# A two-layer network on groups of four row tiles: 512 rows stream in layer 1, layer 2's quantised weights stay in DRAM and come in half-column passes

## The chip, the cores and the metric

The kernel runs on one core of a Trainium2 chip. TensorE (PE in the profile) multiplies matrices, with PEld its weight loads; VectorE (DVE), ScalarE (ACT) and GpSimd (POOL) do the element-wise work, and SyncE's queue (SP) issues the DMAs. The metric is the device time in microseconds from the first to the last instruction, median of three runs.

## The reference, cut to what matters

```python
def mx_quant(x):                      # blocks of 32 along the last axis share one exponent
    amax = max(abs(block)); scale = exp2(floor(log2(amax)) - 6)
    return clip(round(x / scale), -128, 127) * scale
def mx_linear(x, W, b): return bf16(mx_quant(x) @ mx_quant(W).T + b)
def ffn(inputs):                      # rows of 1024, hidden 4096
    x = bf16(inputs)
    h = layernorm(x) * ln_w + ln_b    # rounded to bf16
    h = mx_linear(h, W1, b1)          # layer 1: 1024 -> 4096
    h = gelu(h)                       # tanh form, rounded to bf16
    h = mx_linear(h, W2, b2)          # layer 2: 4096 -> 1024
    return bf16(x + h)
x = x + tanh(g_xattn) * mixer(ctx, layernorm(x))      # 4096 rows, long convolution per head
x = x + tanh(g_ffn) * ffn(layernorm(x))
```

The hidden row has to be complete before it can be quantised, because the blocks of layer 2's contraction run over all of the 4096 hidden values as they are laid out here (32 chunks of 128 partitions, one hidden value of each chunk in a block). So a group's layer 2 can start only when its last hidden chunk has been through gelu, the maxima and the quantising.

## The kernel before

There are 32 tiles of 128 rows. `mixer_block` computes the convolution part, writes the 32 tiles of x1 to DRAM, quantises layer 2's weights (W2) and stores them in DRAM (`store_w2`, L228), and prepares the input of the first four tiles (`EARLY`) for layer 1. It ends near 1029 us. `ffn_block` then runs the network on groups of `GROUP` = 2 tiles, 16 groups of 256 rows. Everything is written out by hand: each engine has its own list of instructions in a fixed order, and semaphores join the lists. No scheduler moves anything.

- **TensorE**: `layer1(g, b)` (L961) computes two of 32 hidden chunks, each with 8 matmuls of 256 streamed columns, into one of four PSUM buffers (`L1_BANKS`). `layer2(t, part)` (L976) takes the quantised hidden tile as stationary operand and streams 512 columns of the resident W2; 64 matmuls a tile, 128 a group. The first two groups' layer 1 is interleaved with a lag of 11 buffers (`LAG`), then comes layer 2 of group 0, layer 1 of group 2, layer 2 of group 1, and so on: a group's layer 1 stands one group ahead of layer 2.
- **ScalarE**: `add_bias` (L1022) empties PSUM, `gelu` (L1029) works on quarters of the hidden tile (128 x 2048 elements), `first_norm` (L1001) normalises the input of a later tile, `norm_again` (L1009) the residual.
- **VectorE**: W1's 16 weight tiles are quantised while the first layer 1 runs (`weight_ints` L1199, `weight_scales` L1203, `weight_clip` L1208, `weight_quant` L1213); tile j releases hidden chunks 2j and 2j+1. `peak` (L1134 to L1146) takes the maxima of a quarter, `hidden_scales` and three instructions (L1162, L1167, L1172) quantise a group, `first_statistics` (L1065 to L1078), `second_statistics`, `weigh_input` and `quantise_input` (L1094 to L1124) make a later tile's input, `second_bias` and `gated_sum` (L1180, L1183, L1189) finish a tile of output.
- **GpSimd**: one or two tiny powers and products per tile (L1268, L1270), between `first_statistics` and `first_norm`.
- **SP queue**: W1's raw tiles through six places, W2 once into `w2_T` (8 MB, resident), x1 tiles, the transposing DMAs of the inputs (`turn_input`), output stores.

At the head of each list stands what the next group needs. Two places of the lists matter below. In VectorE's weight loop the maxima wait for gelu:

```python
                if j in (7, 11):
                    peak(0, j // 4 - 1)
```

and on ScalarE each group's list ends with the norms of the tiles two groups on, ahead of the next group's `add_bias`:

```python
                for s in range(GROUP):
                    if g + 2 < groups:
                        first_norm(GROUP * (g + 2) + s)
```

## Time and profile before

| | us |
|---|---|
| median of three runs | 1991.64 (1991.03 to 1994.72) |
| the profiled execution | 1993.12 |
| its span in the trace | 1991.2 |
| first layer 1 matmul starts | 1031.5 |
| last layer 2 matmul ends | 1984.9 |
| PE busy, DVE busy, ACT busy | 1900.2 (95%), 1695.3 (85%), 755.8 (38%) |

A row of the page's groups names line, engine and operation, output and inputs, count, busy time and mean duration. In the trace's timeline each row has start, duration and, in brackets, how long the engine sat idle and who released it. The chain that ended last lists start and length of each link. PEclk is the granted TensorE clock, 1.00 is 2.4 GHz and 0.50 is 1.2 GHz; a value in between is a mean over the stretch.

### The profile page before, as it was taken

To read this page: it belongs to the slowest core of one execution; us is meant where nothing else is said; L and a number is where in the kernel's file an instruction comes from. 1 tells how busy PE (TensorE), PEld (TensorE's weight loads), DVE (VectorE), ACT (ScalarE), POOL (GpSimd) and SP (SyncE) were. 2 spreads that over 40 slices of the span, in tenths; PEclk is the share of its full clock that TensorE was granted. 3 is DMA by queue.
4 is the path that set the end of the run, shared out by engine and by line. 5 is a ranking of instruction groups with operands and counts; after the bars stand their busy time and mean duration, and the time that the engine had idled before them with its cause. 6 is when DMAs were issued, how large, how long until landed. Compare 5 with 4: busy or idle time off the path is not lost. (4 is left out here: it accounts for less than half of the span.)

```text
span 1991.2 us, 29456 instructions
## 1 busy us (share of the span) xinstructions
PE 1900.2 (95%) x11632; PEld 1499.2 (75%) x11680; DVE 1695.3 (85%) x2082; ACT 755.8 (38%) x1036; POOL 955.9 (48%) x1028
## 2 busy tenths in 40 slices
PE   6999999999999999999966959999999999999998
PEld 5988888888898988899854736667777666666773
DVE  6899999998898888988889798988888888898843
ACT  4333333333334333333303524444554444445440
POOL 3888899888899999999940000000000000000000
PEclk9999999999999999999978979999999999999999
DMA  6554445665645554655448312212221212211112
GB/s 247 186 179 157 156 155 202 210 224 217 220 173 168 183 195 153 217 175 193 144 174 321 129 43 75 75 49 69 75 75 69 70 53 64 75 61 57 54 43 74
DMA packets 99274, 271.75 MB, mean 136 GB/s; under 512 B 41472, under 2 KB 41472, under 8 KB 90944
## 3 DMA queue, kind: packets, MB, share of 16 engines
q1 hardware_dynamic: 99136, 269.86, 39.4%
q8 instruction: 92, 1.51, 0.3%
q14 instruction: 46, 0.38, 0.1%
HBM read 218.91 MB, written 42.53 MB: 131 GB/s over the span
## 5 line engine op out<-in xcount | busy, mean ns | idle before, releaser
L318 PE MATMUL y_ps<-kk_hi,slab 128*128 128x352 f32 (+6 forms) x3328 | 895.4, 351 | 21.7 <-DMA slab<-taps_scratch 18.4
L318 PEld LDWEIGHTS y_ps<-kk_hi,slab 128*128 128x128 f32 x3328 | 595.2, 189 | 90.4 <-issue 22.4
L318 PE MATMUL y_ps<-kk_lo,slab 128*128 128x512 f32 (+6 forms) x1664 | 580.9, 349 | 0.0
L976 PE MATMUL acc_ps<-w_T,arena 128*128 128x512 bf16 x2000 | 439.5, 379 | 2.5
L961 PE MATMUL l_ps<-f_xq_T,w_T 128*128 128x256 bf16 x3584 | 399.1, 275 | 21.4 <-ACT arena L1022 16.7
L961 PEld LDWEIGHTS l_ps<-f_xq_T,w_T 128*128 128x128 bf16 x3584 | 353.1, 99 | 68.3 <-ACT arena L1022 17.0
L976 PEld LDWEIGHTS acc_ps<-w_T,arena 128*128 128x128 bf16 x2048 | 200.3, 98 | 238.6
L1268 POOL TENSOR_TENSOR f_rstd<-f_var_eps,f_neg_half 128x1 f32<-128x1 f32 x28 | 15.3, 548 | 706.6 <-DVE f_var_eps L1078 706.6
L318 PEld LDWEIGHTS y_ps<-kk_lo,slab 128*128 128x128 f32 x1664 | 314.2, 189 | 34.2
L1022 ACT ACTIVATE arena<-l_ps,f_b 128x256 bf16<-128x256 f32 x512 | 213.8, 472 | 246.6 <-PE l_ps L961 241.2
L509 DVE TENSOR_TENSOR upper<-y_ps,q_ext 128x768 f32<-128x768 f32 (+1 forms) x128 | 156.0, 1218 | 96.5 <-PE y_ps L318 90.8
L748 POOL TENSOR_TENSOR lsum<-lower 128x240 f32<-128x240 f32 x127 | 169.1, 1332 | 65.8 <-DVE lower L515 65.6
L749 POOL TENSOR_TENSOR upper<-upper 128x384 f32<-128x384 f32 x127 | 183.5, 1445 | 0.0
L381 ACT COPY k_ps<-k_ext 128x512 f32<-128x512 f32 x64 | 37.9, 592 | 381.3 <-DVE kk L489 378.9
L495 DVE TENSOR_TENSOR kk_lo<-kk,kk_hi 128x2304 fp32r<-128x2304 f32 x64 | 172.4, 2694 | 6.1 <-ACT kk_hi L395 5.9
L760 POOL TENSOR_TENSOR mixed<-upper 128x192 f32<-128x192 f32 x127 | 158.4, 1247 | 18.5 <-POOL upper L757 0.4
L395 ACT CAST kk_hi<-kk 128x2304 fp32r<-128x2304 f32 x64 | 136.2, 2128 | 9.6 <-DVE kk L489 7.6
L1001 ACT ACTIVATE f_n<-arena,f_shift,f_rstd 128x1024 bf16<-128x1024 f32 x28 | 34.6, 1240 | 244.9 <-POOL f_shift L1270 244.9
L1029 ACT ACTIVATE arena<-arena 128x2048 bf16<-128x2048 bf16 x64 | 121.8, 1909 | 0.5
L515 DVE TENSOR_TENSOR lower<-y_ps,q_ext 128x576 f32<-128x576 f32 (+1 forms) x128 | 121.2, 947 | 0.0
L751 POOL TENSOR_TENSOR lsum<-lsum,lower 128x240 f32<-128x240 f32 x127 | 119.0, 937 | 0.0
L486 DVE TENSOR_TENSOR kk<-k_ps,k_ext 128x1536 f32<-128x1536 f32 x64 | 111.8, 1747 | 0.7 <-ACT k_ps L381 0.7
(135 smaller groups left out, 2062.9 us busy)
## 6 DMA issues: line engine op xcount, KB each, us to landing
slab<-taps_scratch SPq DMA_DIRECT2D x128, 512.0 KB, 4.7
arena<-in_w_m SPq DMA_DIRECT2D x32, 1024.0 KB, 6.3
arena<-x_scratch SPq DMA_DIRECT2D x60, 512.0 KB, 3.8
k_ext<-in_ctx_e SPq DMA_DIRECT2D x64, 384.0 KB, 3.4
arena<-in_w SPq DMA_DIRECT2D x18, 1024.0 KB, 6.8
x_tile<-in_x_t SPq DMA_DIRECT2D x32, 512.0 KB, 6.3
out_t<-arena SPq DMA_DIRECT2D x32, 512.0 KB, 2.6
x_scratch<-x SPq DMA_DIRECT2D x31, 512.0 KB, 4.5
```

Of the source, the lines that this page charges most:

```text
L318: mm = nc.tensor.matmul(y_ps[:, y_base + begin:y_base + end], slab[s][:, half, d * P:(d + 1) * P], kk_part[s][:, begin - d * PAIR:end - d ...
L395: nc.scalar.copy(kk_hi[h % 2][:], kk[:].rearrange("p n c -> p (n c)")).then_inc(hi_ready, 1)
L495: nc.vector.tensor_tensor(kk_lo[h % 2][:], kk[:].rearrange("p n c -> p (n c)"), kk_hi[h % 2][:].bitcast(F32), ALU.subtract).then_inc(lo_re ...
L509: nc.vector.tensor_tensor(view(up, 0, [((DIAG + 1) * CH, count), (CH, DIAG), (1, CH)]), view(y_ps, y_at, [(PAIR, count), (CH, DIAG), (1, C ...
L515: nc.vector.tensor_tensor(view(low, B, [(3 * ACCW, count), (ACCW + B, 3), (1, CH)]), view(y_ps, y_at + CH, [(PAIR, count), (CH, 3), (1, CH)]),
L748: add(lsum[:, :, B:], low[:, :, 0, B:], low[:, :, 1, B:], ALU.add).then_inc(lower_two, 1)
L749: add(up[:, :, 0:2, :], up[:, :, 0:2, :], up[:, :, 2:4, :], ALU.add).then_inc(upper_two, 1)
L760: add(out, rows[0], rows[4], ALU.add).then_inc(sums_ready, 1)
L961: mm = nc.tensor.matmul(l1_ps[bank % L1_BANKS][:, a, :], w1_T[:, b, k, a * P:(a + 1) * P], inputs[:, k, :], start=(k == 0), stop=(k == L / ...
L976: mm = nc.tensor.matmul(acc_ps[s][:, c * 512:(c + 1) * 512], hidden[g % 2][:, k, s * P:(s + 1) * P], w2_T[:, k, c * 512:(c + 1) * 512], st ...
L1022: done = nc.scalar.activation(hidden[g % 2][:, c, :], l1_ps[bank % L1_BANKS][:, a, :], ACT.Identity, bias=b1_c[:, c:c + 1])
L1029: nc.scalar.activation(h, h, ACT.Gelu_apprx_tanh).then_inc(gelu_ready, 1)
```

## The change

The network works on groups of four tiles, so there are 8 groups of 512 rows. `mixer_block` is the same but for `store_w2`, which stores each quantised W2 tile as two half-column pieces, and the place where the early inputs are put.

- Layer 1 computes one hidden chunk with 8 matmuls of 512 columns into one PSUM bank of 512 floats; two sets of four banks take turns between groups. There is no interleaving of groups 0 and 1: the order is layer 1 of group 0, both passes of layer 2 of group 0, layer 1 of groups 1 and 2, layer 2 of group 1, layer 1 of group 3, and so on.
- Layer 2 runs in two passes of half the output columns over four tiles; eight pieces of W2 of 512 KB per pass come from DRAM into six places (`w2_slots`), for group 0 into twelve. The last pass goes tile by tile. Output is finished in units of 128 rows by 512 columns.
- Gelu and the maxima work on eighths of the hidden group, again 128 x 2048 elements. The quantising goes in two halves of the rows, 128 x 32 x 256 each.
- In the weight loop six maxima stand instead of two.

The core of the diff (the lists of VectorE and SP for groups 0 and 1 are written out by hand in the same way and are left out):

```diff
-GROUP = 2
-EARLY = 2 * GROUP
-LAG = 11
+GROUP = 4
+EARLY = GROUP
+HALF = L // 2
-L1_BANKS = 4
+BANKS = 4
+EIGHTHS = 8
...
             def store_w2(j):
                 done = last_stored if j == W_TILES - 1 else w2_stored[j % 3]
                 sp.wait_ge(w2_quant, j + 1)
-                sp.dma_start(w2_q[j], w2_raw[j % 3][:, 0:L].bitcast(BF16)).then_inc(done, 16)
+                quantised = w2_raw[j % 3][:, 0:L].bitcast(BF16).rearrange("p (k c o) -> p k c o", k=2, c=2)
+                for c in range(2):
+                    sp.dma_start(w2_q[c, j // 2, :, j % 2 * 2:j % 2 * 2 + 2, :], quantised[:, :, c, :]).then_inc(done, 16)
...
+            def layer1(g):
+                for c in range(chunks):
+                    if g == 0:
+                        pe.wait_ge(quant_ready, c // 2 + 1)
+                    if g >= 1 and c == 0:
+                        for done in input_turned:
+                            pe.wait_ge(done, 32 * g)
+                    if c >= BANKS:
+                        pe.wait_ge(biased, chunks * g + c - BANKS + 1)
...
                     for k in range(L // P):
-                        mm = nc.tensor.matmul(l1_ps[bank % L1_BANKS][:, a, :], w1_T[:, b, k, a * P:(a + 1) * P], inputs[:, k, :],
-                                              start=(k == 0), stop=(k == L // P - 1))
+                        mm = nc.tensor.matmul(banks[g % 2][c % BANKS][:], w1_T[:, c // 2, k, c % 2 * P:(c % 2 + 1) * P],
+                                              inputs[g][:, k, :], start=(k == 0), stop=(k == L // P - 1))
...
+            layer1(0)
+            layer2(0, 0)
+            layer2(0, 1)
+            layer1(1)
+            for g in range(2, groups):
+                layer1(g)
+                layer2(g - 1, 0)
+                layer2(g - 1, 1)
+            layer2(groups - 1, 0)
+            last_pass()
...
+            for c in range(chunks):
+                add_bias(0, c)
+                if c >= 5 and c % eighth == 1:
+                    gelu(0, c // eighth - 1)
...
+            for g in range(1, groups):
+                t = GROUP * (g + 1)
+                units_left = 8 * (g - 2) + 6 if g >= 3 else 6 if g == 1 else 0
+                for c in range(chunks):
+                    add_bias(g, c)
...
+                    if c == 15 and t < tiles:
+                        first_norm(t + 2)
+                    if c == 19 and t < tiles:
+                        first_norm(t + 3)
+                gelu(g, EIGHTHS - 1)
+                if g >= 2:
+                    for n in range(6):
+                        norm_again(8 * (g - 1) + n)
+                if t + GROUP < tiles:
+                    first_norm(t + 4)
+                    first_norm(t + 5)
...
-                if j in (7, 11):
-                    peak(0, j // 4 - 1)
+                if j >= 4 and j % 2 == 0:
+                    peak(0, j // 2 - 2)
```

On ScalarE, in the stretch in which W1 is quantised, the list before has ten biases of 256 columns (five weight tiles' worth of chunks) ahead of the first gelu, then eight and ten ahead of the next two (`arena` holds the hidden group, `l_ps` is PSUM):

```order
L1022 ACTIVATE arena<-l_ps,f_b 128x256 x10
L1029 ACT_TABLE_LOAD
L1029 ACTIVATE arena<-arena 128x2048
L1022 ACTIVATE arena<-l_ps,f_b 128x256 x8
L1029 ACTIVATE arena<-arena 128x2048
```

and the changed one (`hidden` is the hidden group, `bank` is PSUM) has six biases of 512 columns, then four before each gelu:

```order
L1179 ACTIVATE hidden<-bank,f_b 128x512 x6
L1185 ACT_TABLE_LOAD
L1185 ACTIVATE hidden<-hidden 128x2048
L1179 ACTIVATE hidden<-bank,f_b 128x512 x4
L1185 ACTIVATE hidden<-hidden 128x2048
```

The first gelu, and with it the first maxima, moved from the fifth weight tile to the third. On VectorE, in the same stretch, the changed list has maxima (L1302 to L1314) behind every second weight tile; two weight tiles between one set of maxima and the next read:

```order
L1367 TENSOR_TENSOR f_o_res<-arena 128x2048
L1382 TENSOR_TENSOR w_T<-arena,w_scale 128x2048
L1372 TENSOR_SCALAR w_scale<-arena 128x256
L1377 TENSOR_SCALAR f_o_res<-f_o_res 128x2048
L1367 TENSOR_TENSOR arena<-arena 128x2048
L1382 TENSOR_TENSOR w_T<-f_o_res,w_scale 128x2048
L1372 TENSOR_SCALAR w_scale<-arena 128x256
L1377 TENSOR_SCALAR arena<-arena 128x2048
L1302 TENSOR_SCALAR f_weighted<-hidden 128x2048
L1305 TENSOR_TENSOR f_weighted<-f_weighted 128x1024
L1312 TENSOR_TENSOR f_weighted<-f_weighted 128x512
L1314 TENSOR_TENSOR f_amax_h<-f_amax_h,f_weighted 128x512
```

Before, four weight tiles stood between the two sets. On ScalarE, at the end of layer 1 of group 1 in the changed kernel, the norms (`f_n<-f_xin`) of tiles 12 and 13 stand between the last gelu of group 1 and the first bias of group 2:

```order
L1185 ACTIVATE arena<-arena 128x2048
L1164 ACTIVATE f_n<-f_xin,f_shift,f_rstd 128x1024 x2
L1179 ACTIVATE hidden<-bank,f_b 128x512 x6
```

and on VectorE the statistics (`f_stats<-f_xin`) of these tiles stand behind the quantising of both halves of group 1:

```order
L1334 TENSOR_TENSOR arena<-arena,f_inv_h 128x32x256
L1337 TENSOR_SCALAR arena<-arena 128x32x256
L1339 TENSOR_TENSOR arena<-arena,f_scale_h 128x32x256
L1334 TENSOR_TENSOR arena<-arena,f_inv_h 128x32x256
L1337 TENSOR_SCALAR arena<-arena 128x32x256
L1339 TENSOR_TENSOR arena<-arena,f_scale_h 128x32x256
L1235 BN_STATS f_stats<-f_xin 128x6
```

On TensorE the two layer 1 blocks of 256 matmuls, groups 1 and 2, stand side by side there:

```order
L1120 MATMUL bank<-arena,hidden 128x512 x16
L1094 MATMUL bank<-w_slots,w_T 128x512 x256
L1094 MATMUL bank<-arena,w_T 128x512 x256
L1120 MATMUL bank<-w_slots,arena 128x512 x256
```

In the kernel before the same place had layer 2 of a group of two tiles between two such blocks, half as long.

## Rows read from the trace of the kernel before

**Rows 1.** Stretches: length, busy PE, PEld, DVE, ACT, POOL (x), granted clock, DMA, GB/s.
```profile
1031.50:1124.60 93.10, 67.99 (x513) 54.00 (x515) 83.83 (x91) 34.15 (x69) 0.74 (x2) 0.85 0.73 277
1124.60:1234.80 110.20, 88.55 (x508) 52.59 (x513) 96.72 (x156) 38.65 (x51) 7.47 (x16) 0.88 0.19 58
1234.80:1984.90 750.10, 747.88 (x5079) 500.51 (x5118) 596.58 (x882) 323.96 (x519) 28.75 (x67) 1.00 0.20 65
```
**Rows 2.** Chain that ended last: start, length, engine, line; one steady group, and the end.
```profile
1234.80 27.95 PE l_ps L961 x256
1262.80 10.74 PE acc_ps L976 x49
...
1290.38 27.95 PE l_ps L961 x256
...
1984.92 1.24 DVE f_o_res L1180
...
1986.91 1.28 DVE arena L1189
```
**Rows 3.** Timeline of TensorE: weight stage, and both stalls behind it.
```profile
1066.57 3.42 PE L961 MATMUL l_ps<-arena,w_T 128*128 128x256 bf16 x16 [4.27 <-DVE w_T L1213]
1070.65 1.92 PE L961 MATMUL l_ps<-arena,w_T 128*128 128x256 bf16 x16 [0.66 <-DVE w_T L1213]
...
1156.81 9.58 PE L961 MATMUL l_ps<-f_xq_T,w_T 128*128 128x256 bf16 x64 [4.67 <-issue]
```
**Rows 4.** Stretches behind the second stall: TensorE's matmuls at either clock.
```profile
1183.10:1188.60 5.50, 5.48 (x26) 3.93 (x27) 4.87 (x8) 5.12 (x10) 0.55 (x1) 0.50 0.02 8
1190.00:1195.00 5.00, 5.00 (x48) 4.49 (x46) 4.79 (x10) 2.27 (x7) 0.00 (x0) 1.00 0.00 0
```
**Rows 5.** Timeline of VectorE in the weight stage: maxima, then weight tiles.
```profile
1060.97 0.69 DVE L1134 TENSOR_SCALAR f_weighted<-arena 128x2048 uint16<-128x2048 uint16 x1
...
1063.10 2.28 DVE L1199 TENSOR_TENSOR arena<-w_T,arena 128x2048 int16<-128x2048 f32 x1
1065.30 1.22 DVE L1213 TENSOR_TENSOR w_T<-f_o_res,w_scale 128x2048 bf16<-128x2048 int16 x1
...
1067.17 2.28 DVE L1199 TENSOR_TENSOR f_o_res<-w_T,arena 128x2048 int16<-128x2048 f32 x1
```
**Rows 6.** Timeline of ScalarE: first gelu's table load, a pair of biases, a gelu.
```profile
1056.39 1.28 ACT L1029 ACT_TABLE_LOAD   x1
...
1103.59 0.84 ACT L1022 ACTIVATE arena<-l_ps,f_b 128x256 bf16<-128x256 f32 x2 [0.91 <-PE l_ps L961]
1104.46 1.91 ACT L1029 ACTIVATE arena<-arena 128x2048 bf16<-128x2048 bf16 x1
```
**Rows 7.** Timeline of VectorE: scales, quantising, one tile's input, statistics.
```profile
1108.97 0.23 DVE L1150 TENSOR_SCALAR f_amax_h<-f_amax_h 128x256 bf16<-128x256 bf16 x1
...
1109.89 4.42 DVE L1162 TENSOR_TENSOR arena<-arena,f_inv_h 128x8192 int16<-128x8192 bf16 x1
...
1121.02 0.69 DVE L1065 BATCH_NORM_STATS2 f_stats<-arena 128x6 f32<-128x512 f32 x1
...
1122.65 0.14 DVE L1078 TENSOR_SCALAR f_var_eps<-f_mean_var 128x1 f32<-128x1 f32 x1
...
1137.12 1.28 DVE L1094 SCALAR_TENSOR_TENSOR f_weighted<-f_n,f_neg_mean,lnw_b 128x1024 f32<-128x1024 bf16 x1
...
1144.23 0.69 DVE L1134 TENSOR_SCALAR f_weighted<-arena 128x2048 uint16<-128x2048 uint16 x1
```
**Rows 8.** The stall at 1183 us: ScalarE's norms, then TensorE.
```profile
1179.41 1.24 ACT L1001 ACTIVATE f_n<-arena,f_shift,f_rstd 128x1024 bf16<-128x1024 f32 x1 [43.44 <-POOL f_shift L1270]
...
1183.12 7.14 PE L961 MATMUL l_ps<-f_xq_T,w_T 128*128 128x256 bf16 x37 [16.72 <-ACT arena L1022]
```
**Rows 9.** DMA issues from 1005 us on: count, KB each, median us to landing.
```profile
arena<-x_scratch SPq DMA_DIRECT2D x60, 512.0 KB, 3.8
out_t<-arena SPq DMA_DIRECT2D x32, 512.0 KB, 2.6
...
f_xq_T<-f_hq SPq DMA_TRANSPOSE x28, 3.1
```

More of the change, by code:

```diff
@@ L793, in ffn_block @@
     nb1 = L // QB
-    banks = HID // P // 2
-    quarter = HID // P // 4
-    first_banks = []
-    for b in range(banks + LAG):
-        first_banks += [(0, b)] if b < banks else []
-        first_banks += [(1, b - LAG)] if b >= LAG else []
-    def number(g, b):
-        return banks * g + b if g >= 2 else first_banks.index((g, b))
+    chunks = HID // P
+    eighth = chunks // EIGHTHS
+    half_rows = rows // 2
+    units = []
+    for g in range(groups):
+        for part in range(2):
+            for u in range(BANKS):
+                if g == 0:
+                    c, tile = (u // 2) ^ part, u % 2
+                    units.append((2 * part + tile, c, 1 - part, 2 * c + tile))
+                else:
+                    units.append((GROUP * g + u, part, (g + part + (g == groups - 1)) % 2, u))
@@ new lines, in ffn_block @@
+    first_buffers = (10, 11, 6, 7, 12, 13, 0, 1, 2, 3, 8, 9)
+    first_uses = [(c, first_buffers[c % 12]) for c in range(16)]
+    first_uses += [(c, first_buffers[c % 12]) for c in range(4, 16)] + [(c, first_buffers[4 + c]) for c in range(4)]
+    first_uses = [(c // W_CHUNKS, c % W_CHUNKS, b) for c, b in first_uses]
+    uses = {(0, 0): first_uses[:16], (0, 1): first_uses[16:]}
+    n = 0
+    for g in range(1, groups):
+        for part in range(2):
+            last = g == groups - 1 and part == 1
+            uses[g, part] = []
+            for c in range(W_CHUNKS):
+                if last and c < 2:
+                    uses[g, part].append((part, c, 14 + c))
+                else:
+                    uses[g, part].append((part, c, n % 6))
+                    n += 1
@@ L804, in ffn_block, with loads_needed, load_signal @@
+    def loads_needed(b, here):
+        pair = [b] if b < 6 else [b & ~1, b | 1]
+        before = len([k for k in uses_of(b) if use_number(*k) < here and not (k[:2] == (0, 1) and k[2] < 12)])
+        return 16 * len(pair) * (before + 1)
+    def load_signal(b):
+        return b if b < 6 else 3 + b // 2
     with ExitStack() as stack:
@@ L1062, in _ @@
+            for n in range(8 * (groups - 2) + 6, 8 * groups):
+                norm_again(n)
         @block.vector
         def _(dve):
+            done = {"peaks": 0, "inputs": 0}
             def mean_var(src, out, stat_done, aggr_done, t):
@@ L1185, in gated_sum @@
[L1185 to L1196 removed]
+                                        ALU.bitwise_and).then_inc(h_scaled, 1)
@@ L1260, in _ @@
+            for n in range(8 * (groups - 2) + 4, 8 * groups):
+                second_bias(n)
+                gated_sum(n)
         @block.gpsimd
```

758 lines of the change are left out of this document (458 added, 300 removed).

## The prediction

> **What bounds the kernel now.** I read the stretches of the network first [rows 1]. From 1234.8 us to the end TensorE is busy for 747.9 of 750.1 us at full clock. The two stretches ahead of that are different: 93.1 us with 68.0 busy (and clock 0.85), 110.2 us with 88.6 busy. So TensorE's work bounds the steady part, and the start of the network is bounded by something else. Up to 1031.5 us the change touches only the stores of W2.
>
> The chain of waits gives the steady pace [rows 2]: a group of two tiles starts every 55.58 us (1234.80 to 1290.38), 28.00 for 256 matmuls of 256 columns (0.109 each) and 27.58 for 128 matmuls of 512 columns (0.2155 each). Sixteen groups are 889.3 us. From 1031.5 to 1984.9 are 953.4, so 64.1 us are lost, all of it ahead of 1234.8.
>
> The timeline shows how: in the weight stage TensorE waits for VectorE's weight tiles, and after a gap of 4.27 us its 16 matmuls take 3.42 us, after a gap of 0.66 us 1.92 [rows 3]. Later it idles 4.67 us, and 64 matmuls then take 9.58 instead of 7.0. The granted clock explains both: behind the second stall it is 0.50 (1.2 GHz) for 5.5 us with 26 matmuls, 0.21 us each, then 1.00 (2.4 GHz) with 48 in 5.0 us [rows 4]. So a restart costs about 2.6 us on top of the gap, and TensorE is cold for some 5 us. The second stall is 16.72 us: layer 1 of group 2 has filled its four buffers, and ScalarE, which should empty them, sits 43.44 us in front of a norm whose statistics VectorE makes only behind the quantising of group 1 [rows 8].
>
> **The wide matmul.** Layer 1 with 512 columns should run at layer 2's pace: 2048 x 0.2155 = 441.3 instead of 16 x 28.00 = 448.0, a gain of 6.7 us. The granted clock is full in both, so I see no other source of gain. A pass over four tiles is then 256 x 0.2155 = 55.2 us; all of TensorE's work 16 x 55.16 = 882.6.
>
> A page speaks against this price: the Trainium skill, "TensorE: Matmul & The Clock Gate", section "Back-to-back issue gap", says that N = 512 sustains about 131 ns per matmul and that 216 ns is the isolated gap. The rows contradict it here, with 0.2155 us over whole passes; what its rule would give is the fourth rival below.
>
> **The weight stage.** VectorE takes 4.07 us for a weight tile (1063.10 to 1067.17) and 2.13 for the first maxima (1060.97 to 1063.10); from the start of a tile's first instruction it is 2.20 to its last, which lasts 1.22 [rows 5], so TensorE starts 3.5 us after the maxima. With the same number of instructions but two of them twice as wide I take 2.36 for a set of maxima, 1.85 for a group's first, which has one fewer. Before, four weight tiles stand between sets and the chunks needed are long done. Now a set stands behind every second tile, and it needs the second chunk of the tile quantised just after the previous set. From the end of one set: 3.5 until TensorE has the tile, the matmuls, 0.2 until ScalarE sees the result, 0.65 for the bias, 1.9 for gelu, 2.36 for the maxima. A bias of 512 columns isn't in the trace; it lies between one of 256 (0.42) and two (0.84) [rows 6], and 0.65 is nearer to two, because most of it is columns. The matmuls take 16 x 0.2155 = 3.45 at full clock, 6.8 at 1.2 GHz, and 5.9 if the clock rises after 5 us. Full clock gives a period of 12.05, and TensorE then idles 4.5 us in each: longer than the gap of 4.27 that left it cold. So I take 5.9 and a period of 14.5, with 5.2 us of idle time in it. VectorE's own work is 8.14 + 2.36 = 10.5: it now waits 4 us per pair.
>
> The first set: behind tile 4 VectorE is at 1060.97 - 3 x 4.07 = 1048.8. The tile needed, number 2, is ready at 1065.30 - 5 x 4.07 - 2.13 + 1.3 = 1044.1; matmuls 3.45, 0.2, bias 0.65, table load 1.28 [rows 6], gelu 1.9 give 1051.6, and the set ends at 1053.4. Five periods later, 1125.9. Then 3.5 + 5.9 + 0.2 + 0.65 + 1.9 give gelu at 1138.05, maxima 1140.4, two tiles' statistics 2 x 1.7 (1121.02 to 1122.79, [rows 7]) 1143.8, last maxima 1146.2, scales 1147.4 (0.92 for 256 columns, 1.2 for 512), and quantising of 8192 elements per partition, 11.1 us [rows 7], with 0.1 for the start. Layer 2 of group 0 starts at **S = 1158.7**. Before, LAG filled this wait with group 1; now TensorE idles about 20 us.
>
> **From S to the full pipeline.** VectorE, in its order: quantising the second half 11.2; two statistics 3.4; a tile's input 7.1 (1137.12 to 1144.23, [rows 7]); statistics 3.4; input 7.1; statistics 3.4; two output units 3.7 (half of 1.24 + 0.70 + 1.28, [rows 2], with fixed parts: 1.85 each); two biases 1.4; input 7.1; statistics 3.4; two unit ends 2.3; input 7.1. That is 60.6. The transposing DMA adds 3.1 [rows 9], so layer 1 of group 1 starts at S + 63.8. Layer 2 of group 0 ends at S + 55.2 + 2.7 = 57.9: a gap of 5.9, and cold again, 2.5.
>
> Within that layer 1, tile 11's norm stands on ScalarE behind chunk 19: S + 63.8 + 2.5 + 34.5 + 0.2 + 0.65 + 1.24 = 102.9. VectorE reaches it at about 93 and waits, which covers its late loads of tiles 10 and 11. Then 1.7, input 7.1, two unit ends 2.3, input 7.1, eight maxima 18.4, scales 1.2, quantising 22.2, two statistics 3.4: S + 166.3. Only now can GpSimd and ScalarE make the norms of tiles 12 and 13, which stand in front of group 2's first bias. From the end of the statistics at 1180.16 to TensorE at 1183.12 were 2.96 [rows 8]. Meanwhile layer 1 of group 2 has done four chunks and filled its banks at about S + 131.5. It resumes at S + 169.3 = 1328.0: **a stall of 38 us**, where 16.7 were before. Twenty-eight chunks are 48.3, cold start 2.7: 1379.0.
>
> Twelve passes follow: 12 x 55.16 = 661.9, to 2040.9. In this part VectorE's work for four tiles, at the same prices, is 98 of 110.3 us, and W2's 8 MB per group are 76 GB/s. Each W2 place is freed at least 10 us before its next piece must have landed, but for the very last, where it is 1 to 2. I price the stream at nothing; the pieces land behind the matmuls. If that cover went, each late piece would cost its 3 to 7 us.
>
> The end: from 1984.7 to the span's end were 6.5; with half the columns in VectorE's last three instructions 1.4 less, 5.1. Span 2046.0, and 1.9 around it (1993.12 - 1991.2): 2047.9 against 1993.12 of the same execution, 1.5 above the median. **Predicted 2046.5.** As a check: lost time grows from 64.1 to 126.8, less 6.7 and 1.4, is 54.6 us.
>
> W2's stores are cut into pieces of 1 KB instead of 4, sixteen DMAs more on SP. In the trace no instruction of TensorE waits for a slab late in the mixer, so I take 0, with -1 to +4 as bounds.
>
> **Rivals.**
> 1. *The weight stage doesn't go cold, or doesn't wait for gelu.* For it: the clock was at 1.00 in the tiles after short gaps [rows 3], and here TensorE is busy for more of each period. Full clock: 5 x 2.45 + 2.45 = 14.7 less, 2032. No wait at all: S 25 earlier, 2021.5.
> 2. *The group boundary slips.* After a group's layer 1 ends (T), VectorE ends its second unit pair at T + 49.3; two stores and two reloads in series on SP (2.6, 2.6, 3.8 from the first's end, [rows 9]), norms and the first bias reach T + 61.0; TensorE's banks are full at T + 62.1. Only 1 us is left. If the reloads land 1 to 4 us later, each of five boundaries costs up to 3: 2061.
> 3. *W2's stream collides* with tile loads and stores behind in-order waits of SP, most likely in group 0, where twelve places are filled during the weight loads. Against it: DMA share 0.20 in the steady part [rows 1]. 5 to 20 us: 2059.
> 4. *Faster than before.* One mechanism: the wide matmul streams faster than 0.2155 in both layers. It decides from 55 / 4096 = 0.013 us less per matmul if VectorE follows; but VectorE's 98 us per group is then the floor, 12 less in each of six groups, and the start stays. At 131 ns (the page's number) that is 2046.5 - 72 = 1974. The row of layer 2 is 0.2155 in every steady group, so this is remote.
>
> **How the numbers follow.** Forecast (cold weight stage, 38 us stall, clean boundaries) 0.52; rival 1 0.24; rival 2 0.14; rival 3 0.07; rival 4 0.03. The range leaves out rival 4 and what is beyond either end of the others: 2021 to 2062. A measurement of this kernel can tell about 0.2% (4 us) from no change. All cases but the last are over 25 us slower: faster 0.03, same 0.01, slower 0.96.
>
> **What would show it.** Six sets of maxima about 14.5 us apart, each with VectorE idle in front released by ScalarE, and granted clock 0.5 at every restart: right for the weight stage; 10.5 apart would be the low end. Layer 2's first matmul near 1159. One idle time of TensorE near 1290 to 1328, released by ScalarE's bias, with ScalarE released by GpSimd just before: right for the stall; if the norms come before group 2's chunks, the main term falls. Layer 1 passes of 55.2 us; full clock and no gap from 1379 on; gaps at each pass's start would be rivals 2 or 3.

## The result, and the profile after

The changed kernel takes 2059.31 us (median of 4 runs, 2057.64 to 2060.94) where the kernel before takes 1992.33: a ratio of 1.0333, with a 95% interval of 1.0320 to 1.0345. The forecast was 2046.5 with a range of 2021 to 2062. The profiled execution took 2060.94, with a span of 2058.8.

The timeline of TensorE in the changed kernel, which answers to [rows 3] and [rows 8] (start, length, engine, line, operation; in brackets the idle time ahead and what ended it). L1094 is layer 1, L1120 is layer 2, L1139 the second half of the output columns in the last group. A pass below is 256 matmuls, one layer of one group; in layer 2 it has two halves:
```profile
1099.25 8.77 PE L1094 MATMUL bank<-arena,w_T 128*128 128x512 bf16 x32 [4.83 <-DVE w_T L1382]
...
1154.77 11.88 PE L1120 MATMUL bank<-arena,hidden 128*128 128x512 bf16 x47 [19.55 <-DVE hidden L1339]
...
1219.95 22.02 PE L1094 MATMUL bank<-w_slots,w_T 128*128 128x512 bf16 x87 [8.41 <-issue]
...
1287.17 8.77 PE L1094 MATMUL bank<-arena,w_T 128*128 128x512 bf16 x32 [6.05 <-issue]
1329.46 51.05 PE L1094 MATMUL bank<-arena,w_T 128*128 128x512 bf16 x219 [33.52 <-ACT hidden L1179]
1380.34 55.42 PE L1120 MATMUL bank<-w_slots,arena 128*128 128x512 bf16 x251
...
1990.15 20.88 PE L1120 MATMUL bank<-w_slots,arena 128*128 128x512 bf16 x94 [0.36 <-issue]
2018.17 8.50 PE L1120 MATMUL bank<-w_slots,arena 128*128 128x512 bf16 x31 [7.14 <-DMA w_slots<-w_scratch]
```
In the weight stage TensorE waits 4.83 us for VectorE every 13.6 us. It idles 19.55 us before layer 2 of group 0, and 33.52 us behind the first four chunks of group 2, released by ScalarE's bias. From 1380.34 to 1990.15 eleven passes follow at 55.4 us each. At the very end stands a wait that the forecast hadn't: 7.14 us for a piece of W2.

The same as stretches, as in [rows 1] (length, then busy PE, PEld, DVE, ACT, POOL, granted clock, DMA share, GB/s):
```profile
1034.30:1126.50 92.20, 59.46 (x220) 23.69 (x224) 72.03 (x82) 30.54 (x36) 0.00 (x0) 0.89 0.61 233
...
1287.20:1380.30 93.10, 59.36 (x251) 26.04 (x257) 74.82 (x114) 37.24 (x42) 6.88 (x12) 0.80 0.09 31
1380.30:1435.60 55.30, 55.04 (x253) 25.05 (x257) 51.20 (x61) 6.45 (x7) 1.48 (x4) 1.00 0.51 148
```
Work that takes 55 us in the third stretch takes 93 in the second. From TensorE's first matmul of layer 1 (1034.26) to the end of the last one of layer 2 (2054.30) are 1020.0 us; 16 passes of 55.16 are 882.6; so 137.4 us are lost, where the kernel before lost 64.1 and the forecast had 126.8.

Against the forecast, in the order of time (the forecast's own steps, each measured from the step ahead):

| step | forecast | measured | difference |
|---|---|---|---|
| first matmul of layer 1 | 1031.5 | 1034.3 | +2.8 |
| from there to layer 2 of group 0 | 127.2 | 120.5 | -6.7 |
| from there until the long stall ends | 169.3 | 174.7 | +5.4 |
| rest of that layer 1 | 51.0 | 50.9 | -0.1 |
| eleven passes | 606.8 | 609.8 | +3.0 |
| last pass, both halves | 55.2 | 64.2 | +9.0 |
| end behind the last matmul | 5.1 | 4.5 | -0.6 |

Together +12.8, from 2046.0 to 2058.8.

### The profile page after: what moved, and what is told of

The parts are those of the page before. It is cut to its first block and busy times, and to the rows that moved or that the text cites. A ratio compares the mean times of both kernels' runs of the same rounds, so it can differ in the third digit from the quotient of the medians.

```text
span 2058.8 us, 25423 instructions
## 1 busy us (share of the span) xinstructions
PE 1901.7 (92%) x9550; PEld 1297.5 (63%) x9632; DVE 1695.5 (82%) x2090; ACT 721.6 (35%) x812; POOL 972.5 (47%) x1028
## 5 line engine op out<-in xcount | busy, mean ns | idle before, releaser
L1094 PE MATMUL bank<-arena,w_T 128*128 128x512 bf16 x1756 | 404.1, 390 | 79.7 <-DVE w_T L1382 37.0
L1094 PEld LDWEIGHTS bank<-arena,w_T 128*128 128x128 bf16 x1792 | 178.3, 100 | 304.6 <-DVE w_T L1382 41.5
L1514 POOL TENSOR_TENSOR f_rstd<-f_var_eps,f_neg_half 128x1 f32<-128x1 f32 x28 | 22.7, 810 | 493.0 <-DVE f_var_eps L1248 493.0
L1120 PE MATMUL bank<-w_slots,arena 128*128 128x512 bf16 x877 | 194.6, 381 | 8.5 <-DMA w_slots<-w_scratch 7.1
L1172 ACT ACTIVATE f_o_res<-arena,f_shift,f_rstd 128x512 bf16<-128x512 f32 x64 | 51.2, 810 | 412.4 <-DMA arena<-x_scratch 412.3
L1120 PE MATMUL bank<-w_slots,hidden 128*128 128x512 bf16 x831 | 182.9, 379 | 0.9
L764 POOL TENSOR_TENSOR mixed<-upper 128x192 f32<-128x192 f32 x127 | 157.7, 1242 | 18.5 <-POOL upper L761 0.4
L1120 PEld LDWEIGHTS bank<-w_slots,arena 128*128 128x128 bf16 x896 | 87.9, 98 | 114.8 <-DMA w_slots<-w_scratch 7.6
L1120 PEld LDWEIGHTS bank<-w_slots,hidden 128*128 128x128 bf16 x848 | 83.0, 98 | 100.0
L1524 POOL TENSOR_TENSOR f_rstd<-f_var_eps,f_neg_half 128x1 f32<-128x1 f32 x28 | 19.8, 707 | 232.7 <-DVE f_var_eps L1255 232.7
```

What stands on the lines that cost most here:

```text
L764: add(out, rows[0], rows[4], ALU.add).then_inc(sums_ready, 1)
L1094: mm = nc.tensor.matmul(banks[g % 2][c % BANKS][:], w1_T[:, c // 2, k, c % 2 * P:(c % 2 + 1) * P], inputs[g][:, k, :], start=(k == 0), sto ...
L1120: mm = nc.tensor.matmul(banks[s][bank][:], hidden[g % 2][:, 4 * chunk + k, tile % GROUP * P:(tile % GROUP + 1) * P], w2_buffers[b][:, k, : ...
L1172: nc.scalar.activation(res[n % 2], xfin[n % 2], ACT.Identity, bias=shift1[:, col:col + 1], scale=rs[:, col:col + 1]).then_inc(n2_ready, 1)
```

## The experiments

My theory was: the time is lost where one engine's in-order list holds a wait ahead of what another engine needs (ScalarE's norms ahead of its biases, VectorE's maxima ahead of its weight tiles, SP's stores ahead of loads). The rival was that VectorE's work is the bound in groups 0 to 3, and that the waits are only the places where its lateness shows. Ratios are to the kernel before, which took 1992.3 to 1993.4 beside them; a kernel's runs spread over 3 to 8 us, so I read nothing into a difference of medians under 2 us.

| kernel | median | ratio, 95% interval |
|---|---|---|
| the change | 2059.31 | 1.0333 (1.0320 to 1.0345) |
| e1_norms | 2058.14 | 1.0325 (1.0309 to 1.0340) |
| e2_maxima | 2037.87 | 1.0222 (1.0205 to 1.0239) |
| e3_warm | 2052.48 | 1.0296 (1.0281 to 1.0312) |
| e4_lastloads | 2057.84 | 1.0323 (1.0307 to 1.0338) |
| e5_norms_loads | 2058.50 | 1.0334 (1.0316 to 1.0351) |
| e6_interleave | 2055.45 | 1.0314 (1.0296 to 1.0332) |
| e7_tiles | 2048.57 | 1.0284 (1.0268 to 1.0299) |
| e8_all | 2018.87 | 1.0134 (1.0119 to 1.0149) |
| e9_sums | 2004.54 | 1.0055 (1.0042 to 1.0068) |
| e10_sums_both | 1999.73 | 1.0034 (1.0022 to 1.0046) |
| e11_reload_norms | 1998.32 | 1.0026 (1.0017 to 1.0035) |
| e12_reload_norms_both | 1997.67 | 1.0028 (1.0017 to 1.0038) |

### The long stall: e1_norms and e5_norms_loads

```
ScalarE, group g:
-  if c == 15: first_norm(t + 2)
-  if c == 19: first_norm(t + 3)
+  later = {23: t, 25: t + 1, 29: t + 2, 31: t + 3} if g == 2 else {15: t + 2, 19: t + 3}
+  if c in later: first_norm(later[c])
   ...
-  if t + GROUP < tiles:
+  if g > 1 and t + GROUP < tiles:
       first_norm(t + 4); first_norm(t + 5)
```


> Edit: in ScalarE's list alone, the first norms of tiles 12 and 13 move from ahead of group 2's first bias to behind its chunks 23 and 25, those of tiles 14 and 15 from behind chunks 15 and 19 to behind 29 and 31. Nothing else moves. Theory (ScalarE's in-order wait at 1325.5 is the whole stall): the 33.5 us in which TensorE waits for ScalarE inside group 2's layer 1 go, layer 2 of group 1 starts some 33 us earlier, and VectorE, which now hands over tiles 12 to 15 later, takes back at most 6 us at the start of group 3's layer 1. Time 2026 to 2032, against 2059.3 of the change. Rival (VectorE's work of groups 1 and 2 is the bound there, and the stall only moves to the next place where TensorE waits for VectorE): 2050 or more, with a stall of over 20 us behind 1340.

The time fell by 1.2 us, which is nothing. TensorE's timeline of e1_norms from the start of group 2's layer 1:
```profile
1285.30 56.93 PE L1094 MATMUL bank<-arena,w_T 128*128 128x512 bf16 x256 [6.34 <-issue]
1342.06 20.88 PE L1120 MATMUL bank<-w_slots,arena 128*128 128x512 bf16 x96
...
1396.36 9.37 PE L1120 MATMUL bank<-w_slots,arena 128*128 128x512 bf16 x32 [12.21 <-DMA w_slots<-w_scratch]
1416.12 9.73 PE L1120 MATMUL bank<-w_slots,arena 128*128 128x512 bf16 x32 [10.39 <-DMA w_slots<-w_scratch]
```
The 33.5 us stall is gone: 256 matmuls run in one piece. But TensorE now waits 12.21 and 10.39 us for pieces of W2. SP's queue in the same kernel says why:
```profile
1358.14 5.15 SPq L962 DMA_DIRECT2D w_slots<-w_scratch  x6
1381.66 10.69 SPq L949 DMA_TRANSPOSE arena<-f_hq  x2
1392.39 1.05 SPq L962 DMA_DIRECT2D w_slots<-w_scratch  x2
```
The two transposing DMAs wait for tiles 14 and 15 from VectorE, and the loads stand behind them. So I moved the loads:
```
SP, group 2:
+  if g == 2: load_layer2(1, 1, 4 .. 7)
   turn_input(t + 2)
   turn_input(t + 3)
-  load_layer2(1, 1, 4), (1, 1, 5); store(8); store(9); load_layer2(1, 1, 6), (1, 1, 7)
+  store(8); store(9)
```


> Edit: that of e1_norms, and in SP's list of group 2 the last four loads of layer 2's pieces for group 1 stand ahead of the transposing DMAs of tiles 14 and 15 in place of behind them and behind two stores. e1_norms took away the 33.5 us wait of TensorE for ScalarE, but TensorE then waited 12.2 and 10.4 us inside layer 2 of group 1 for pieces whose loads SP issued late, and the time fell by 1.2 only. Theory (what ate the gain is SP's list: a transposing DMA waits there for VectorE, with the weights' loads queued behind it; VectorE itself has the time): both waits go, 22 to 24 us below e1_norms, 2033 to 2038. Rival (VectorE's work bounds this stretch, and TensorE waits for tile 15 at the start of group 3's layer 1 or for quantised values behind it): 2045 or more.

That gave nothing either (2058.5 after 2058.1). The timeline of e5_norms_loads:
```profile
1405.67 9.14 PE L1098 MATMUL bank<-arena,w_T 128*128 128x512 bf16 x31 [6.35 <-DVE f_o_res L1353]
1434.46 19.02 PE L1098 MATMUL bank<-arena,w_T 128*128 128x512 bf16 x79 [19.65 <-ACT arena L1183]
```
Both waits for W2 are gone, and 6.35 + 19.65 us stand in group 3's layer 1: there VectorE takes the sums of group 1 late, the stores and reloads follow them, and ScalarE waits for the reloads ahead of its biases. Three times 22 to 34 us, in three places, with ScalarE, a DMA and VectorE named in the brackets. The first theory, that ScalarE's list is the stall, is refuted. What all three places have in common is that VectorE's results come late; that VectorE is the bound is argued here, and tested in e7_tiles and e8_all.

### The weight stage: e2_maxima and e3_warm

```
VectorE, behind weight tile j:
-  if j >= 4 and j % 2 == 0: peak(0, j // 2 - 2)
+  if j >= 5 and j % 2 == 1: peak(0, (j - 5) // 2)
```


> Edit: in VectorE's list alone, in the weight stage, the first six sets of maxima of group 0 stand behind the odd weight tiles 5, 7, ..., 15 in place of 4, 6, ..., 14, which is one weight tile later each. Theory (VectorE waits at each set for ScalarE's gelu, which ends just before; the wait of 2.8 to 5.9 us sets the period of 13.6 us per two weight tiles): the wait goes, the period falls to VectorE's own work, 2 x 4.07 for the tiles and 2.13 for the maxima, 10.3 to 11 us, over six periods some 15 to 18 us, of which the last set of maxima at the stage's end gives back up to 3. Time 2042 to 2046. Rival (the stage is paced by TensorE with a cold clock, 5.9 us per four chunks, or by the weights' loads): less than 5 us, 2054 or more.

It fell by 21.4 us, to 2037.87: more than expected. TensorE in e2_maxima:
```profile
1070.76 3.63 PE L1094 MATMUL bank<-arena,w_T 128*128 128x512 bf16 x16 [2.70 <-DVE w_T L1382]
1074.84 3.63 PE L1094 MATMUL bank<-arena,w_T 128*128 128x512 bf16 x16 [0.45 <-DVE w_T L1382]
1081.16 3.63 PE L1094 MATMUL bank<-arena,w_T 128*128 128x512 bf16 x16 [2.69 <-DVE w_T L1382]
```
The period is 10.40 us (1070.76 to 1081.16), VectorE's own work, and layer 2 of group 0 starts 98.9 us behind the first matmul of layer 1 where it was 120.5.

```
TensorE, group 0, behind chunk c of layer 1:
+  if c % 4 == 3 and 7 <= c < 28:
+      for k in range(14): matmul(bank that nothing holds, ..., 512 columns)
```


> Edit: in group 0's layer 1, behind chunks 7, 11, ..., 27, TensorE gets 14 more matmuls of 512 columns into a bank that nothing holds then; their results are never read, so nothing of the computation changes. They fill the 4.8 us in which TensorE waits for VectorE in each period. Theory (the granted clock falls in that wait, so that the next chunks go at half speed and hand over to ScalarE late, which lengthens the 13.6 us period by what the cold matmuls take longer): the clock stays at 1.00 over 1060 to 1126, the period falls to 12 to 12.5, time 2049 to 2054. Rival (the clock plays no part in the period, since the wait of VectorE for the gelu comes from ScalarE's own work): 2057 to 2061, at a granted clock of 1.00 in that stretch. If the additional matmuls are themselves late, up to 5 us slower.

The time fell by 6.8 us. The same stretch in e3_warm (L1099 are the added matmuls):
```profile
1086.20 3.63 PE L1094 MATMUL bank<-arena,w_T 128*128 128x512 bf16 x16 [1.19 <-DVE w_T L1386]
1090.27 3.63 PE L1094 MATMUL bank<-arena,w_T 128*128 128x512 bf16 x16 [0.45 <-DVE w_T L1386]
1093.74 3.19 PE L1099 MATMUL bank<-arena,w_T 128*128 128x512 bf16 x14
```
Work that nobody uses makes the kernel faster: the period is 11.9 us (1086.20 to 1098.11), the granted clock there 1.00, and 16 matmuls take 3.63 us. The rival, that the clock plays no part, is refuted. In front, VectorE waited 3.4 us for a load of raw weights (1.2 in the changed kernel), which ate part of it: layer 2 of group 0 starts 116.4 us behind the first matmul, 4.1 less. Only these 4.1 us can be put down to the edit; of the rest, 1.9 us are in the last pass, where TensorE's wait for a piece was 4.99 us in this execution and not 7.14.

### The last pieces: e4_lastloads and e6_interleave

```
SP, last group:
+  load_layer2(7, 0, 6); load_layer2(7, 0, 7)
   store(52); store(53); store(54); store(55)
   load_layer2(7, 1, 0); load_layer2(7, 1, 1)
-  load_layer2(7, 0, 6); load_layer2(7, 0, 7)
```


> Edit: in SP's list alone, and in the last group alone, the loads of weight pieces 6 and 7 for the first half of layer 2 stand ahead of stores 52 to 55 in place of behind them. Theory (these two loads are issued at 2010.8 and 2011.7, behind four stores that wait for VectorE; TensorE then waits 7.1 us for them and starts again at half speed): the wait at 2018 and the cold restart behind it go, 8 to 9.5 us, time 2049.5 to 2052. Rival (the pieces' places in the buffer come free late, or the DMA engines are full there, so that they land late anyway): less than 3 us, 2056 or more.

Only 1.5 us came of it. In the trace TensorE's 7.14 us wait is one of 2.62 (for the next piece, which now came last), and its last matmul ends 4.2 us earlier (2.6, counted from each kernel's first matmul of layer 1), but the end behind it is 7.2 us long where it was 4.5: each store and reload came later. So the loads went between the stores:
```
SP, last group:
   store(52); +load_layer2(7, 0, 6); store(53); +load_layer2(7, 0, 7)
   store(54); +load_layer2(7, 1, 0); +load_layer2(7, 1, 1); store(55)
```


> Edit: in SP's list of the last group alone, the loads of pieces 6 and 7 stand behind stores 52 and 53, one each, and the first two loads of the last pass behind store 54. In e4_lastloads both loads stood ahead of all four stores: TensorE's 7.1 us wait fell to 2.6, the last matmul came 4.2 us earlier, but the stores and reloads were all late and the end behind the last matmul grew from 4.5 to 7.2 us. Theory (TensorE's wait for a piece is the price, and the stores lose nothing when the loads stand between them): TensorE's waits go and the end stays within 6 us of the last matmul, 2050 to 2053. Rival (the chain of store, reload, norm and sum through two half-tile buffers bounds the end, whatever TensorE does): TensorE is done 6 us or more earlier and the time is still 2056 to 2059.

The median fell by 3.9 us, half of what the theory says, and its runs (2051.4 to 2059.7) overlap those of the changed kernel (2057.6 to 2060.9), so the size is uncertain. TensorE in e6_interleave (L1142 is the second half of the last pass):
```profile
1990.39 27.79 PE L1123 MATMUL bank<-w_slots,arena 128*128 128x512 bf16 x125 [0.47 <-issue]
2018.01 1.89 PE L1142 MATMUL bank<-arena 128*128 128x512 bf16 x8
2021.75 1.04 PE L1142 MATMUL bank<-w_slots,arena 128*128 128x512 bf16 x4 [1.85 <-DMA w_slots<-w_scratch]
```
The wait of 7.14 us is gone and the second half starts at 2018.0, 8.5 us earlier (7.0 from the first matmul). But its first unit uses a new piece every four matmuls, 0.86 us, and takes 11.7 us (2018.01 to 2029.69) in place of 7.1: now the pieces of this half are late. In the changed kernel no unit of it waits for a piece; they had landed while TensorE waited 7.14 us. The end itself stayed at 4.8 us, so the store chain was no bound here.

### Tiles 10 and 11: e7_tiles

```
SP:
+  load_tile(10); load_tile(11)
   turn_input(7); turn_input(8); load_layer2(1, 0, 0 .. 3)
-  load_tile(10); store(4); store(5); load_tile(11)
+  store(4); store(5)
ScalarE, group 1: first norms of both behind chunks 8 and 10, not 15 and 19
```


> Edit: SP issues the loads of tiles 10 and 11 right behind store 3, ahead of the transposing DMAs of tiles 7 and 8 and of four 512 KB loads of weights, and ScalarE takes their first norms behind chunks 8 and 10 of group 1 in place of 15 and 19. Theory (VectorE's waits of 7.5 and 7.0 us for these two tiles, and 3 us for the norm, lie on VectorE's path to the quantised values of group 1, behind which TensorE's stall ends): layer 1 of group 2 starts up to 6 us earlier and the stall at 1329 ends 8 to 14 us earlier, time 2046 to 2052. Rival (VectorE catches up while it waits for group 1's gelu anyway): layer 1 of group 2 starts earlier, but the stall ends where it did, 2057 to 2060.

The time fell by 10.7 us, as the theory says. Before the edit VectorE waited for both tiles, in the changed kernel:
```profile
1238.46 0.69 DVE L1235 BATCH_NORM_STATS2 f_stats<-f_xin 128x6 f32<-128x512 f32 x1 [7.51 <-DMA f_xin<-x_scratch]
1247.27 0.69 DVE L1235 BATCH_NORM_STATS2 f_stats<-f_xin 128x6 f32<-128x512 f32 x1 [7.04 <-DMA f_xin<-x_scratch]
```
and TensorE in e7_tiles starts group 2's layer 1 without a gap and resumes 10.0 us earlier than in the changed kernel (7.9, counted from each kernel's first matmul of layer 1):
```profile
1282.27 7.07 PE L1094 MATMUL bank<-arena,w_T 128*128 128x512 bf16 x32
1319.46 49.96 PE L1094 MATMUL bank<-arena,w_T 128*128 128x512 bf16 x219 [30.11 <-ACT hidden L1179]
```
This is the other side of e1_norms. The two waits for tiles (14.6 us) were not all: behind them VectorE waited 3.23 us more for tile 11's norm, which stood on ScalarE behind chunk 19. In e7_tiles both tiles come in time, and VectorE waits 4.40 and 2.30 us for the two norms at their new places. So 17.8 us of waiting became 6.7. Taking away TensorE's wait of 33.5 us was worth nothing; taking away these 11.1 us of VectorE's was worth 10.7. The edit moved loads and norms together; neither was tried alone.

### All of it, and how far it goes: e8_all to e12_reload_norms_both

```
+ the edits of e2_maxima, e5_norms_loads, e6_interleave, e7_tiles
VectorE:
-  peak(0, 6); first_statistics(4); first_statistics(5); peak(0, 7)
+  first_statistics(4); first_statistics(5); peak(0, 6); peak(0, 7)
```


> Edit: those of e2_maxima, e5_norms_loads, e6_interleave and e7_tiles together, and VectorE takes the first statistics of tiles 4 and 5 ahead of the last two sets of maxima of group 0, where it waits for a gelu. Nothing else. If the parts add: 2059.3, less 21.4 (measured), less 24 (e5_norms_loads as expected), less 6 to 8, less 4 to 8 (of e7_tiles what isn't the same stall as in e5_norms_loads), less 0 to 3: 1995 to 2004, level with the kernel before. If the parts share one path (VectorE's list over groups 1 to 3), 2010 to 2025.

The time fell by 40.4 us, to 2018.87. That is outside the range for parts that add, because 24 us were counted there for e5_norms_loads, and inside the range for parts that share a path. With what the four gave alone (21.4, 0.8, 3.9, 10.7) the sum is 36.8, so by the measured sizes the parts add; the 3.6 us beyond that, the order of the statistics among them, weren't measured apart.

```
VectorE, group 2:
   prepare(t + 2)
+  second_bias(8); gated_sum(8); second_bias(9); gated_sum(9); second_bias(10); second_bias(11)
+  prepare(t + 3); gated_sum(10); gated_sum(11); first_statistics(16); first_statistics(17)
   peak(2, 7); hidden_scales(2); quantise_hidden(2, 0); quantise_hidden(2, 1)
-  prepare(t + 3) (behind peak(2, 7)) and the other ten (behind or between the two quantise_hidden)
SP: stores 8 and 9 ahead of turn_input(15); ScalarE: norms of 12, 13 at chunks 21, 23, of 16, 17 in group 3
```


> Edit, on top of e8_all: VectorE takes the sums of group 1's first four half tiles, prepares tile 15, and takes the first statistics of tiles 16 and 17 ahead of the two passes that quantise group 2's hidden values, in place of between and behind them; SP's stores and ScalarE's norms follow in that order (norms of tiles 12 and 13 two chunks earlier, those of 16 and 17 behind chunks 2 and 4 of group 3). No work is added or taken away. In e8_all TensorE waited 6.7 us at the start of group 3's layer 1 for VectorE's second bias, and 19.3 us behind chunk 4 for ScalarE, which waited for reloads that follow those sums. Theory (each stall of groups 1 to 3 is an order in the lists of VectorE, ScalarE and SP, and VectorE has idle time there): 18 to 22 us less than e8_all, 1997 to 2001, and no stall over 8 us behind 1200. Rival (VectorE's work up to there is the bound, and layer 2 of group 2 then waits for the quantised values): at most 8 us less, 2011 to 2019, with a new stall of over 10 us between 1400 and 1450.

14.3 us less: short of the theory's 18 to 22, and more than the rival's 8 at most. (Tile 15 was prepared ahead of the quantising before too; here it moves ahead of the last maxima.) The 19.3 us behind chunk 4 of group 3 are gone, but a stall of 13.02 us stands some seven chunks on. It ends with ScalarE's bias and not with the quantised values that the rival names:
```profile
1401.20 39.23 PE L1107 MATMUL bank<-arena,w_T 128*128 128x512 bf16 x165 [13.02 <-ACT arena L1192]
```
```
VectorE, group 0: -gated_sum(2); -gated_sum(3); prepare(7); +gated_sum(2); +gated_sum(3)
SP: turn_input(7) and the loads of tiles 10 and 11 ahead of stores 2 and 3
```


> Edit, on top of e9_sums: in group 0 too, VectorE prepares tile 7 ahead of the sums of half tiles 2 and 3 (it waited 3.9 us for ScalarE there), and SP issues tile 7's transposing DMA and the loads of tiles 10 and 11 ahead of stores 2 and 3. Theory (TensorE's 10.4 us wait at the start of group 1's layer 1 is that order's too): 4 to 6 us less than e9_sums, of which ScalarE's waits for the later reloads may give back 2. Rival (the reloads come so late that layer 1 of group 1 stalls for ScalarE by as much): within 2 us of e9_sums.

4.8 us less, as expected; the gap at the start of group 1's layer 1 fell from 10.84 to 3.61 us, and ScalarE's late reload gave back 3.69.

```
ScalarE, group 3: norm_again(14), norm_again(15) behind chunks 16 and 18, not 6 and 8
```


> Edit, on top of e10_sums_both: in ScalarE's list of group 3 alone, the two norms of reloaded half tiles stand behind chunks 16 and 18 in place of 6 and 8. In e10_sums_both ScalarE waited there 17.1 us for a reload that follows VectorE's sums (1389 us), with the biases of group 3 queued behind it, and TensorE waited 13.0 us for them. Theory (that in-order wait is the whole stall): 11 to 13 us less than e10_sums_both, 1986 to 1989, below the kernel before by 0.2 to 0.35%. Rival (VectorE, with group 3's prepares now late, stalls TensorE at a later group's start): at most 5 us less, 1995 or more.

The 13.0 us stall is gone, and the time fell by 1.4 us, which can't be told from nothing. TensorE in e11_reload_norms:
```profile
1363.48 34.70 PE L1107 MATMUL bank<-arena,w_T 128*128 128x512 bf16 x157
1401.67 4.45 PE L1107 MATMUL bank<-arena,w_T 128*128 128x512 bf16 x10 [3.49 <-ACT arena L1192]
...
1412.93 13.99 PE L1107 MATMUL bank<-arena,w_T 128*128 128x512 bf16 x63 [1.39 <-ACT arena L1192]
...
1493.34 49.87 PE L1107 MATMUL bank<-arena,w_T 128*128 128x512 bf16 x220 [3.49 <-ACT hidden L1192]
```
It is broken up: 3.49, 1.39 and 3.49 us, with a slow restart behind the two of 3.49. The rival holds, and the stretch 1299 to 1486 of this kernel shows what the rival is (columns as above):
```profile
1299.00:1486.00 187.00, 180.46 (x810) 81.24 (x826) 179.35 (x269) 59.98 (x68) 14.36 (x23) 0.98 0.43 135
```
VectorE is busy for 179.35 of 187.00 us (157.89 in the changed kernel), and the view of its waits has not one entry there: the rest lies between its instructions. So in this stretch VectorE is the bound, and an order that only moves waits from one list to another gives nothing. TensorE is as full: 180.46 us. Its 6.5 idle us and the slow restarts are all that is left to gain there.

```
ScalarE, group 1: norm_again(4), norm_again(5) behind chunks 3 and 4, not ahead of the first bias
```


> Edit, on top of e11_reload_norms: in ScalarE's list, the norms of the reloaded half tiles 4 and 5 stand behind chunks 3 and 4 of group 1 in place of ahead of its first bias, where ScalarE waited 11.2 us for the reload and TensorE 3.7 us for ScalarE. Theory (a wait taken away there moves all that follows): 2.5 to 3.7 us less than e11_reload_norms. Rival (VectorE is the bound of group 1 and sets where group 2's layer 1 resumes): within 1 us of e11_reload_norms.

No difference (0.7 us), as the rival says: TensorE's wait in the same layer is 4.54 us where it was 5.37.

None of these kernels beats the kernel before; the best two are 0.26% and 0.28% above it. Where this leaves the change, by the two traces: from the first matmul of layer 1 to the end of the last one of layer 2, e11_reload_norms takes 957.0 us (1031.66 to 1988.66), 74.4 more than the 882.6 of work; the kernel before takes 953.4, of which 64.1 are lost. The wide matmul saves its 6.7 us; the groups of four tiles lose 10.3 more, with the best order found: 70.1 in the eight passes up to 1543.05, 6 more than before, and 4.3 behind them, most of it waits for pieces in the last pass. That no better order exists isn't shown.

### What VectorE waited for

The waits of VectorE over the network's start, in the changed kernel from 1034 to 1490 us, grouped (line, waiting for: us in total, times, longest):
```profile
DVE f_weighted L1302 <- ACT hidden L1185: 37.9, 11, 5.9
DVE f_stats L1235 <- DMA f_xin<-x_scratch: 18.8, 4, 7.5
DVE f_stats L1235 <- ACT f_n L1164: 3.7, 2, 3.2
```
and in e11_reload_norms from 1031 to 1490 us:
```profile
DVE f_stats L1250 <- ACT f_n L1177: 14.6, 4, 7.8
DVE arena L1382 <- DMA w_slots<-in_w: 1.9, 1, 1.9
DVE f_weighted L1317 <- ACT hidden L1198: 1.2, 1, 1.2
```
All entries together are 68.4 and 18.5 us: 49.9 us less waiting of VectorE, of 61.0 us between the two medians. Of the remainder 4 are the last pieces (e6_interleave); what the other 7 are wasn't measured apart.

The same sum from 1031 to 1490 us goes with the time through the series: 69.3 us in the changed kernel, 68.9 and 71.5 in e1_norms and e5_norms_loads, which gained nothing, 64.6 in e7_tiles, 55.6 in e2_maxima, 38.7 in e8_all, 26.4 in e9_sums, 21.6 in e10_sums_both. It counts only where TensorE starves: the kernel before has 48.3 us of such waits, 30.4 of them behind 1235, where TensorE is full all the same.

## Why the prediction was right, and where it was off

**The direction and the main terms held.** The forecast was some 55 us over the kernel before, measured are 67.0. Its two big terms are in the trace: the weight stage waits for gelu, cold, and a stall behind four chunks of group 2 ends with ScalarE's bias. The chain behind that stall (41.72 us is ScalarE's idle time, the norm's statistics come from VectorE through GpSimd) is the one the prediction names:
```profile
1325.51 1.24 ACT L1164 ACTIVATE f_n<-f_xin,f_shift,f_rstd 128x1024 bf16<-128x1024 f32 x1 [41.72 <-POOL f_shift L1516]
```
**The stall** was forecast at 38 us and is 33.5. It ends 174.7 us behind S, the start of layer 2 of group 0, and not 169.3. The mis-sized term is the wait for tile 11's norm, which ends at S + 107.5 and not at S + 102.9, 4.6 of these 5.4 us:
```profile
1261.03 1.23 ACT L1164 ACTIVATE f_n<-f_xin,f_shift,f_rstd 128x1024 bf16<-128x1024 f32 x1
1262.29 0.69 DVE L1235 BATCH_NORM_STATS2 f_stats<-f_n 128x6 f32<-128x512 bf16 x1 [3.23 <-ACT f_n L1164]
```
The norm stands behind chunk 19 of group 1. Layer 1 of group 1 started 1.4 us later than forecast (S + 65.2), and TensorE then waited 1.82, 0.30 and 0.47 us in it for biases, which stood behind norms of reloaded half tiles on ScalarE, where it waited 5.68 and 1.97 us for the reloads. The prediction has no term for that. Its sentence that the wait for the norm covers the late loads of tiles 10 and 11 holds: VectorE waited 7.51 and 7.04 us for them (SP issues them behind transposing DMAs and four 512 KB loads, tile 11 behind two stores too), and still 3.23 for the norm.

One step of the mechanism did not hold. The prediction says that if the norms of tiles 12 and 13 come before group 2's chunks the main term falls, so it takes TensorE's stall for the cost. e1_norms took the stall away and the time stayed. The end of the stall was worked out from VectorE's list, and that is why the number came out: the lateness is VectorE's, and the stall is one place where it shows.

**The weight stage** was forecast at a period of 14.5 us and is 13.6, one of ScalarE's and one of VectorE's rows beside TensorE's above give its steps:
```profile
1095.77 2.28 DVE L1367 TENSOR_TENSOR f_o_res<-arena 128x2048 int16<-128x2048 f32 x1
...
1107.12 0.69 DVE L1302 TENSOR_SCALAR f_weighted<-hidden 128x2048 uint16<-128x2048 uint16 x1 [3.11 <-ACT hidden L1185]
```
```profile
1104.60 0.69 ACT L1179 ACTIVATE hidden<-bank,f_b 128x512 bf16<-128x512 f32 x1 [1.24 <-PE bank L1094]
```
From the end of a set (1095.77) to TensorE (1099.25) 3.48, forecast 3.5; to the bias of the second chunk (1104.60) 5.35, forecast 6.1; bias and gelu 2.52, forecast 2.55; maxima 2.25, forecast 2.36. The one step that is off is the cold matmuls: 16 in 5.15 us, not 5.9, at a mean clock of 0.67, and full clock behind them:
```profile
1099.25:1104.40 5.15, 5.15 (x16) 2.01 (x17) 4.76 (x6) 0.69 (x1) 0.00 (x0) 0.67 0.78 259
1104.40:1108.00 3.60, 3.60 (x17) 1.47 (x15) 0.85 (x2) 3.06 (x3) 0.00 (x0) 1.00 0.52 209
```
Five periods give -4.5 of the -6.7; the rest is an earlier first set (1.3) and a shorter end (1.0). The sign given for it, clock 0.5 at every restart, is right only for the first matmuls. The first half of rival 1, in which nothing goes cold, is about what e3_warm made: 4.1 us up to S, 6.8 in the medians, against 14.7 forecast for it. Its other half, no wait at all, is e2_maxima: 21.4 against 25.

**The last group** is the term that was missed, +9.0. The prediction says that each W2 place is freed in time but the very last. The places were free; the loads were late. SP's queue in the changed kernel:
```profile
1991.15 0.34 SPq L975 DMA_DIRECT2D out_t<-arena  x1
...
2010.43 0.32 SPq L970 DMA_DIRECT2D arena<-x_scratch  x1
2010.79 0.91 SPq L962 DMA_DIRECT2D arena<-w_scratch  x2
2011.74 15.29 SPq L962 DMA_DIRECT2D w_slots<-w_scratch  x8
```
Four stores and four reloads, each waiting for VectorE or a landing, stand from 1991.15 to 2010.43 ahead of the loads; layer 2 is through with the pieces before them at 2011.0. That is rival 3's mechanism (a piece of W2 behind SP's in-order waits), which I gave 0.07 and placed in group 0, where it didn't occur. The prediction priced the stream at nothing; what has a price is its place in the list. In the eleven passes ahead the stream costs nothing that shows: no wait for a piece, and in the first of them DMA share 0.51 and granted clock 1.00.

**The passes**, +3.0: 55.25 us each where 55.16 were forecast is 1.0 of it, waits of 0.24 to 0.41 us at a few chunks the rest. Rival 2 (boundaries slipping by up to 3 us each) did not come. The wide matmul came out as taken: 55.25 us for 256 is 0.2158 us each, in layer 1 too, so rival 4 fell. By the rule of the Trainium skill, "TensorE: Matmul & The Clock Gate", section "Back-to-back issue gap", it would be 131 ns; the trace disagrees in every pass.

**The mixer**, +2.8: over the thirteen traces of the changed kernel and its variants, which have the same mixer, the first matmul of layer 1 comes between 1030.1 and 1034.3 us, at 1032.3 in the mean. So 2.0 us are this one execution, which is chance, and 0.8 are left for the term; against the one trace of the kernel before (1031.5) that can't be told from nothing.

By chance, too, the misses partly cancel: -6.7 in the weight stage stands against +5.4 and +9.0, and the forecast is 12.8 us off where the terms are off by 27.6 in all.

## What to carry to other kernels

Before costing or removing the longest wait of the busiest engine, look at the waits of the engine that feeds it. A stall that several lists could cause moves from list to list (here 22 to 34 us, behind ScalarE's, then SP's, then VectorE's and ScalarE's lists) while the feeding engine comes no earlier. Here the start of the network got shorter where VectorE waited less. In a queue that issues in order, price each stream by what stands ahead of each of its DMAs, in the last round too, and not by its bytes. A group twice as large makes layer 1's matmul wider (0.2158 us in place of two of 0.109), which saves little here, and it doubles what must be done before the next stage can start.
